# Last seven steps of a 64-step attention stage written out in one order per engine, with second buffers and the last three probability tiles transposed on TensorE

## The reference, cut to what matters

```python
x = x + _L0_xattn_ref(_layernorm(x), ctx_4096, ...)
x = x + _L0_ffn_ref(_layernorm(x), ...)
# third stage, for each of 8 batch rows of 128 tokens, 32 heads of 128
q = rmsnorm((h @ q_proj_w.T) per head); k = rmsnorm(...); v = ...
attn = softmax(q k^T * scale + mask); out = (attn v) @ o_proj_w.T
x = x + _L1_xattn_ref(...)
# fourth stage
x = x + (silu(h @ gate) * (h @ up)) @ down
```

## Time and profile before

| | us |
|---|---|
| median of 3 runs | 858.44 (857.34 to 859.26) |
| time of the profiled execution | 859.67 |
| span of the profiled execution | 858.0 |
| TensorE (PE) busy | 822.0 (96%) |
| VectorE (DVE) busy | 565.8 (66%) |
| ScalarE (ACT) busy | 536.5 (63%) |
| GpSimd (POOL) busy | 553.5 (65%) |
| share of TensorE in the chain that ended last | 83% |

### The profile page before, as it was taken

One profiled execution on the slowest core, in us unless ns is written; L12 is line 12 of the kernel. 1 busy time (PEld: TensorE's weight loads), 2 busy tenths in 40 slices (PEclk: granted clock), 3 DMA queues, 4 the chain that ended last, 5 costly groups with the idle time before them and its releaser, 6 DMA issues.

```text
span 858.0 us, 13297 instructions
## 1 busy us (share of the span) xinstructions
PE 822.0 (96%) x3920; PEld 673.7 (79%) x3920; DVE 565.8 (66%) x990; ACT 536.5 (63%) x1769; POOL 553.5 (65%) x557
## 2 busy tenths in 40 slices
PE   6899999999899999999999999999997899999995
PEld 4687888788788888888888888888885677777773
DVE  5606752533566666666666666666666789999996
ACT  4543561144777777777776777776675467777763
POOL 3332562321577777777777777777776258999995
PEclk9999999999999999999999999999999999999999
DMA  7511567203566666666667766667654123343302
GB/s 269 179 50 29 143 164 203 66 1 111 165 205 194 186 185 186 185 186 186 187 188 223 224 192 188 180 194 227 187 159 120 52 74 147 147 148 148 141 7 99
DMA packets 99350, 131.34 MB, mean 153 GB/s; under 512 B 25998, under 2 KB 71950, under 8 KB 99279
## 3 DMA queue, kind: packets, MB, share of 16 engines
q1 hardware_dynamic: 99278, 130.49, 50.3%
HBM read 90.61 MB, written 39.85 MB: 152 GB/s over the span
## 4 chain that ended last, share of the span: by engine, by line
PE 83%; DVE 6%; DMA 4%; ACT 2%; POOL 2%; issue 1%; SPq 1%; POOLq 0%; DVEq 0%; ACTq 0%
PE pair L1433 19%; PE pair L1435 19%; PE pair L1434 19%; PE pair L1591 8%; PE pair L1592 8%; PE pair L1685 6%; DMA land<-block_bounce 2%; DMA block_bounce<-tb 1%; PE pair L1453 1%; DVE kv L1302 1%; DMA resid<-in_x_dram 1%; PE pair L1492 1%; PE pair L1543 1%; PE pair L1548 1%; PE pair L1520 1%
## 5 line engine op out<-in xcount | busy, mean ns | idle before, releaser
L1433 PE MATMUL pair<-split,xnT_hi 128*128 128x512 f32 x288 | 113.3, 394 | 0.3 <-issue 0.3
L1435 PE MATMUL pair<-split,xnT_lo 128*128 128x512 f32 x288 | 112.1, 389 | 0.0
L1434 PE MATMUL pair<-split,xnT_hi 128*128 128x512 f32 x288 | 112.1, 389 | 0.0
L909 ACT ACTIVATE headT<-land,wqk 128x512 f32<-128x512 f32 x64 | 46.3, 724 | 89.8 <-DMA land<-block_bounce 60.8
L1433 PE MATMUL pair<-split,aoT_hi 128*128 128x512 f32 x256 | 101.3, 396 | 0.0
L934 ACT ACTIVATE prob<-pair,nmax 128x128 f32<-128x128 f32 x256 | 90.3, 364 | 17.3 <-DVE nmax L1269 16.5
L1435 PE MATMUL pair<-split,aoT_lo 128*128 128x512 f32 x256 | 100.9, 394 | 0.0
L1434 PE MATMUL pair<-split,aoT_hi 128*128 128x512 f32 x256 | 100.5, 393 | 0.0
L704 POOL TENSOR_TENSOR prob<-prob,rinv 128x512 f32<-128x512 f32 x64 | 66.7, 1043 | 43.9 <-DVE rinv L1239 43.9
L1591 PE MATMUL pair<-xnT_hi,split 128*128 128x512 f32 x224 | 91.3, 408 | 3.3 <-ACT kv L1000 1.3
L1592 PE MATMUL pair<-xnT_lo,split 128*128 128x512 f32 x224 | 88.5, 395 | 0.0
(11 more groups left out here) (152 smaller groups left out, 2135.5 us busy)
## 6 DMA issues: line engine op xcount, KB each, us to landing
block_bounce<-tb SPq DMA_DIRECT2D x244, 128.0 KB, 2.3
land<-block_bounce SPq DMA_DIRECT2D x61, 512.0 KB, 3.2
raw<-in_wqo_dram SPq DMA_DIRECT2D x62, 256.0 KB, 2.9
kv<-in_ffn_w_dram SPq DMA_DIRECT2D x14, 768.0 KB, 4.4
kv<-in_ffn_z_dram SPq DMA_DIRECT2D x14, 768.0 KB, 5.7
kv<-key_bounce SPq DMA_DIRECT2D x32, 128.0 KB, 2.7
key_bounce<-tb SPq DMA_DIRECT2D x44, 64.0 KB, 2.0
resid<-in_x_dram SPq DMA_DIRECT2D x2, 1024.0 KB, 9.6
```

The lines of the kernel that those rows point to most:

```text
L1433: pe.matmul(dst, l_hi, r_hi, start=first, stop=False)
L1434: pe.matmul(dst, l_hi, r_lo, start=False, stop=False)
L1435: return pe.matmul(dst, l_lo, r_hi, start=False, stop=last)
```

## The change

Up to turn 57 (`DRAIN`, that is `STEPS - 7`) nothing moves, except that ScalarE leaves its loop one turn earlier (its turn 57 is written out) and that the copy for unit 0's down weights and the subtraction for unit 1's gate weights move later. From there each engine has an order of its own, written out:

- A second buffer for attended products, probabilities and values, in the free end of the weight buffer `split[:, 1]`, is used by even steps from 58 (attended) and from 60 (the other two). Attend of steps 61 and 63 goes to bank 2, the output product of step 62 to bank 5.
- The probabilities of steps 61, 62 and 63 (`TURNED` is 61) are not sent through DRAM. TensorE transposes them in four 128x128 transposes each (into banks 4, 0 and 1), ScalarE copies the high part out of PSUM, VectorE makes the low part (before, GpSimd). VectorE's block transposes of these three and the last three writes and reads of the round trip are gone.
- Steps 58 to 63 on TensorE now are: scores 62, attend 59, transpose 61, out 58, scores 63, transpose 62, out 59, attend 60, attend 61, transpose 63, out 60, attend 62, ln transposes 0 and 1, out 61, attend 63, ln transposes 2 and 3, out 62, out 63, ln transposes 4 and 5, then unit 0's first gate products.
- The first gate products stand behind all output products (before, between those of steps 62 and 63), and banks of the ln transposes are renumbered.

```diff
+DRAIN = STEPS - 7
+TURNED = STEPS - 3
...
+        def spare(a, n):
+            return split[:, 1, UW + a:UW + a + n]
+
+        def attended(i, part):
+            if i > DRAIN and i % 2 == 0:
+                return spare(part * D, D)
+            return (aoT_hi, aoT_lo)[part][:]
+
+        def probs(i, part):
+            if i > DRAIN + 2 and i % 2 == 0:
+                return spare((2 + part) * D, D)
+            return (probT_hi, probT_lo)[part][:]
...
+        def attend_bank(i):
+            return bank[2 if i >= TURNED and i % 2 else 6]
+
+        def out_product_bank(i):
+            return bank[5 if i == STEPS - 2 else 7]
+
+        def turn_bank(i):
+            return bank[(4, 0, 1)[i - TURNED]]
...
-                if 0 <= j + LEAD - 1 < STEPS + PLAG:
+                if 0 <= j + LEAD - 1 < STEPS:
                     bounce_read(j + LEAD - 1)
...
-                if j + LEAD < STEPS + PLAG:
+                if j + LEAD < STEPS:
                     bounce_write(j + LEAD)
...
+            sub_gate(1, None)
+            probs_normed(STEPS - 2)
+            values_lo(STEPS - 4)
...
+            values_lo(STEPS - 3)
+            sub_up(1, None)
+            probs_normed(STEPS - 1)
+            values_lo(STEPS - 2)
+            ln_rstd(3, 0)
+            values_lo(STEPS - 1)
...
+            def probs_hi(i):
+                if i < TURNED:
+                    act.wait_ge(s_br, 16 * (i + PLAG + 1))
+                    act.activation(by_head(probs(i, 0)), landed(i + PLAG, 1), ACT.Copy).then_inc(s_pt, 1)
+                else:
+                    act.wait_ge(s_pp, i - TURNED + 1)
+                    act.activation(probs(i, 0), turn_bank(i), ACT.Copy).then_inc(s_pt, 1)
...
+            def probs_transpose(i):
+                pe.wait_ge(s_pn, i + 1)
+                if i > TURNED:
+                    pe.wait_ge(s_sq, i + 1)
+                for h in range(REP):
+                    done = pe.transpose(turn_bank(i)[:, tile(h)], prob[:, tile(h)], ident[:])
+                done.then_inc(s_pp, 1)
...
+            def out_product(i):
+                pe.wait_ge(s_al, i + 1)
+                if i != STEPS - 2:
+                    pe.wait_ge(s_add, T + i if i < STEPS - 2 else T + i - 1)
...
+            scores(STEPS - 2)
+            attend_values(STEPS - 5)
+            probs_transpose(STEPS - 3)
+            out_product(STEPS - 6)
...
+            out_product(STEPS - 2)
+            out_product(STEPS - 1)
...
             for t in range(HALF, HALF + 2):
                 ln_transpose(3, t)
+            pe.wait_ge(s_ug, 1)
+            pe.wait_ge(s_xlo, 3 * T + HALF)
+            for k in range(KT):
+                first(0, 0, k, k)
+            ln_transpose(3, T - 2)
             pe.wait_ge(s_uu, 1)
```

More of the change, by code:

```diff
@@ L917, in step @@
                         .then_inc(s_vh, 1)
-                if p is None and j == STEPS - 3:
-                    for t in range(2):
-                        ln_hi(3, t)
                 if valid(j + 2):
@@ L958, in down_ready @@
                 ready(i, p, DOWN, 2, s_ud)
-            for j in range(-LEAD, STEPS):
+            for j in range(-LEAD, DRAIN):
                 step(j, None)
@@ new lines, in exps @@
+            def exps(i):
+                act.wait_ge(s_mx, i + 1)
+                if i <= TURNED:
+                    act.wait_ge(s_tp, i)
+                else:
+                    act.wait_ge(s_pp, i - TURNED)
+                for h in range(REP):
+                    done = act.activation(prob[:, tile(h)], bank[2 + i % 2][:, tile(h)], ACT.Exp,
+                                          bias=nmax[:, h:h + 1], accum_out=rsum[:, h:h + 1])
+                done.then_inc(s_ex, 1)
+            attended_hi(DRAIN)
@@ new lines, in _ @@
+            values_hi(STEPS - 2)
+            probs_hi(STEPS - 2)
+            attended_hi(STEPS - 4)
+            attended_hi(STEPS - 3)
+            act.wait_ge(s_ri, STEPS)
+            act.activation(rsum[:, 0:1], rsum[:, 0:1], ACT.Silu)
+            values_hi(STEPS - 1)
+            probs_hi(STEPS - 1)
+            gate_ready(1, None)
+            attended_hi(STEPS - 2)
+            for t in range(2):
+                ln_hi(3, t)
+            attended_hi(STEPS - 1)
+            for t in range(2, HALF):
+                ln_hi(3, t)
@@ L1697, in attend @@
                         .then_inc(s_e, 1)
-                if p is None and j == STEPS - 3:
-                    for t in range(2):
-                        ln_transpose(3, t)
                 if valid(j + 1):
@@ new lines, in out_product @@
+            def out_product(i):
+                pe.wait_ge(s_al, i + 1)
+                if i != STEPS - 2:
+                    pe.wait_ge(s_add, T + i if i < STEPS - 2 else T + i - 1)
+                b = WO_BUF[i // T % 2]
+                for h in range(REP):
+                    done = three(out_product_bank(i), attended(i, 0)[:, tile(h)], attended(i, 1)[:, tile(h)],
+                                 wbuf(b, 0)[:, h, :], wbuf(b, 1)[:, h, :], h == 0, h == REP - 1)
+                done.then_inc(s_f, 1)
@@ L1740, in _ @@
-            first(0, 1, 3, 6)
             pe.wait_ge(s_xlo, 4 * T)
```

246 lines of the change are left out of this document (182 added, 64 removed).

## The result

The changed kernel takes 850.39 us (median, 850.15 to 850.66), the kernel before, run beside it, 858.1 us. The ratio is 0.9904 (95% interval 0.9891 to 0.9916). The forecast was 850.4.

The account below looks back on a forecast made before the run. TensorE's waits in a hand-over from 640 to 690 us, where no engine is full, were the target; the new order ended it 685.04 - 677.0 = 8.0 us earlier, so 858.44 - 8.0 = 850.4 us, range 847.4 to 854.3.

Parts of the forecast that it names:

- the hand-over: Stretch from 640 to 690 us, between attention and last stage: no engine full, TensorE idle for 9.55 us.
- The layout: New order on old durations from scores 62 at 643.37: last low part ends at 677.0 instead of 685.04, 8.0 us saved.
- Rival A: The new order's placing holds within its unknowns: gain 6.3 to 9.7 us, forecast 8.0; chance 0.62.
- the tie: At transpose 61, input ready at 644.9 and TensorE arriving at 645.0, so no wait.
- the second clock fall: TensorE's slow clock from 686 to 689 us, costing 1.6 us; left standing in the forecast.
- rival C: Slow clock at 686 to 689 goes (1.0) and normalized tile 7 is quick (0.8): gain 9.8 to 11 us; chance 0.12.
- The tile 7: VectorE's last normalized tile, taken at 1.35 us as before; at 0.48 the gain would grow by 0.8 us.
- The sum from the other side: Cross-check: 9.55 of waits, 1.6 slow clock, some 0.5 restarts, less three transposes and new waits, leaves 7.7 us.
- the wait of 2.89: TensorE's wait before attend 61, put down to step 60's attended copy queued behind step 63's exponentials; an order can mend it.
- rival B: Clock falls in new places, likely after waits around 654 to 661, or near-ties slip: gain 3.5 to 6.3 us; chance 0.18.
- Rival D: Softmax chain in TensorE's list stalls all of TensorE; decides if each of three transpose waits grows by 2.7 us; chance 0.05.
- Rival E: Last stage held by its weights, unit 2's asked for later, so no gain: 858.4 us; chance 0.03.

Follow-up runs that it names:

- the repeats: The changed kernel run twice more, unaltered: 850.85 us (ratio 0.9903) and 849.26 us (0.9898) against the kernel before.
- edit (a): Changed kernel, GpSimd's first sum for unit 0 held until VectorE's last normalized tile is made: 849.03 us alone, 848.76 us with two order swaps added.
- The idle multiplications: The kernel before with matmuls that nobody reads placed in TensorE's waits, two versions: 858.15 us and 857.79 us (ratio 0.9995 each).
- the second idle multiplications: The kernel before with unread matmuls, twelve ahead of attend 61 and eleven about the ln transposes: 857.79 us (0.9995).

## Why the prediction was right, and where it was off

**Where the time goes.** It said that the change works in the hand-over only, and that a microsecond there moves the last stage as a whole. Right: behind the first 128x1024 operation both kernels take the same time but for the chance of 0.8 named above, and the three ratios of the changed kernel (0.9904, 0.9903, 0.9898) are 8.2, 8.3 and 8.8 us. From the start of scores 62 to that operation its three profiles take 42.99, 42.71 and 42.28 us, the kernel before 51.09: 8.1, 8.4 and 8.8 less.

**The layout.** Rival A held, with 7.0 (7.3 and 7.7 in the repeats) inside its 6.3 to 9.7. Taken from the start of scores 62, transpose 61 came 0.99 later than laid out (2.62 instead of 1.63), out 60 0.88 later, ln transposes 4 and 5 0.96 later, ln transpose 7 and the last low part 1.03 and 1.04 later. So what the layout was off by came in at one place. The step that failed is the tie, "TensorE arrives at 645.0, so a tie": it took the exponentials of step 61 to end 0.1 after the start of scores 62, as in the profile of before, in which the writes at 633 had about the shortest issue (1.76). With 3.10 they ended 1.2 after it (the first starts at 642.06, four take 1.5). That term was 0 and measured 0.87, 0.54 and 0 in the three profiles of the changed kernel. The others: scores 63 0.3, measured 0.1; transpose 63 0.4 and 0.30; out 60 0.8 and 0.47; out 61 0.5 and 0.45; ln transpose 7 0.6 and 0.42. The transposes out of `prob`, laid with 0.45 each and named as unknown, took 0.36 and 0.41 until the next product began. The gain in the hand-over was 7.0 where 8.0 were laid out.

**The median hit nonetheless.** The missing 1.0 came back as the 1.1 of the second clock fall, which the forecast had left standing and rival C had priced at 1.0 of its 1.6. So two errors of one microsecond each cancel, and the hit within 0.1 us is luck; the mechanism and the size of 8 are not. One piece stays open: the kernel before has one profile, so how often its executions have that second fall isn't known. Four of the five variants built on it don't have it. Between the two profiles themselves 9.1 us went where 8.0 were forecast, and the difference is the 1.04 ahead of scores 62. The tile 7 took 1.40 (1.35 taken), so the other half of C didn't come; the runs with edit (a) show what would have brought it.

**The sum from the other side** (9.55 of waits, 1.6 of slow clock, 0.5 of restarts) gave 7.7 near the right number, but its terms don't stand for themselves. The idle multiplications took the clock falls away and gained nothing that can be measured (0.9995, 0.9986 to 1.0004). Waits are no such terms either: the buffer part alone cuts attend 61's wait from 2.89 to 1.01 and costs 2.4 us; the transposes alone cost 1.5 by the ratio (0.7 by the medians); both together gain 0. Taken out of the full change, they cost 12 and 2.4. The reason given for the wait of 2.89, the order of ScalarE's list, was one of several that had to be mended together. What was right is the layout, which places each instruction behind its last input.

**The clock.** The granted clock after is 1.00 from 640 to 690 in all three profiles of the changed kernel, with three more transposes in the list than the kernel before, and eight ln transposes. No fall came in a new place of the hand-over, so rival B didn't come. The two repeats have a 0.83 from 830 to 840; that is the chance of 0.8 us named above, which variants of the kernel before show too. The Trainium skill, "TensorE: Matmul & The Clock Gate", Part 4: PE-mode transpose, doesn't count a transpose as activity for the clock. By that rule the eleven tiles transposed in 30 us (644.95 to 674.99) were a reason for 1.2 GHz; here the clock stayed at 2.4 GHz. That doesn't refute the page, since full queues of products stood between them; its rule just had no price in this kernel.

**Rival D** (the chain of softmax in TensorE's own list) had its three waits at 0.87, 0 and 0.30 instead of the 2.7 each from which it decides. With one attended buffer a similar chain did decide, at 862.6. **Rival E** (the last stage held by its weights) fell: from the last low part to the end it is 171.9 us, before 172.96.

**What was to be seen.** The waits between 640 and 690 are 4.5 us in sum, not 2 to 4 (4.2 and 3.7 in the repeats), and one is above 1.0: the 1.20 of unit 1 at 684.01, which the shorter hand-over brought into the window. Up to 680 none is. Out 60 and out 61 were to have the longest; transpose 61 had it.

## What to carry to other kernels

Where several engines take strict lists, lay the whole new order out instruction by instruction from measured durations: a part of such a change can be worth nothing or less alone (860.9, 858.8 and 858.5 against 858.1 to 858.6) and cost 12 us when it is taken out of the whole. Don't add up waits and slow-clock time as if each were to be had. For each near-tie in the layout look how much the late input varies, over the turns of one trace and, for that very turn, over several executions, above all where it comes from a DMA. Here 48 of 67 turns of one trace issued in under 1.8 us, but this turn did so in only three of fourteen profiles. One turn of one profile is a draw, here of 1.1 us.

## What the runs showed of the hardware that was not expected

- A VectorE normalization of one 128x512 tile (TENSOR_SCALAR, fp32, SBUF to SBUF) takes 0.54 to 0.55 us alone and 1.40 (1.35 before) beside GpSimd's TENSOR_TENSOR of the same size, which keeps its 1.29; it ends 0.3 after GpSimd's. The Trainium skill, "SBUF — State Buffer", Who interferes with whom, says that the two engines share a pair of ports, that a `tensor_scalar` can take it in a two-port mode, and that the later of two instructions waits for the whole of the other. The traces agree in kind, not in size: the sum had 1.11 us left when the tile began, and a full wait would give 1.11 + 0.54 = 1.65, 0.25 more than measured. The measurement decides: the tile lost less than a full wait.
- The issue of four DMA writes of one shape takes 1.75 to 3.38 us within one execution, and the same four took 1.75 to 3.23 over fourteen executions.
- In the kernel before the clock fell at 686 after waits of 0.54 and 1.26. After the same three waits of TensorE before the last first products (0.53, 0.54, and 1.26 or 1.27) the clock fell in one kernel (both parts together, 0.63 us matmuls from 684.21) and not in three others (buffer and order only; transposes only; the second idle multiplications). The waits just ahead don't tell it alone, and what else does is open.
